# Large aggregations: products in PSUM and a sum by halves; sort turns in two banks

## The reference

```
x = x + gat0(layernorm(x), edges)        # 8 heads x 32
x = x + moe_small(layernorm(x), edges1)  # experts gated by a small 4 x 4 attention over 131072 edges
x = x + gat1(layernorm(x), edges)        # 4 heads x 64
x = x + moe(layernorm(x))                # 8 experts, the best 2 of each row
```

```
e     = leaky_relu(left[src] + right[dst], 0.2)         # (edges, heads)
p     = exp(e - segment_max(e, dst)[dst])
alpha = p / segment_sum(p, dst)[dst]
out   = segment_sum(table[src] * alpha[:, :, None], dst)  # (nodes, 256)
```

## Time and profile before

| what | value |
|---|---|
| median of three runs | 10248.09 us |
| profiled execution, own time | 10220.8 us |
| its span | 10218.8 us |
| busy: DVE (VectorE) / POOL (GpSimd) | 5655.7 us (55%) / 5738.3 us (56%) |
| busy: PE / ACT (ScalarE) | 2312.4 us (23%) / 1171.8 us (11%) |
| large aggregation 0 | 1000 to 3670 us of the span |
| small aggregation | 4232 to 5800 us |
| large aggregation 2 | 6306 to 8865 us |

### The profile page before, as it was taken

The page is one execution under the profiler, slowest core; times in us unless marked ns, Lnnn a source line. Parts: engine busy times, 40 slices in busy tenths (PEclk is TensorE's granted clock), DMA queues, the critical chain, the costliest instruction groups (busy, mean ns, idle before and its releaser), DMA issues. The chain is left out here.

```text
span 10218.8 us, 56607 instructions
## 1 busy us (share of the span) xinstructions
PE 2312.4 (23%) x9111; PEld 1766.1 (17%) x9112; DVE 5655.7 (55%) x8530; ACT 1171.8 (11%) x2978; POOL 5738.3 (56%) x5411
## 2 busy tenths in 40 slices
PE   0112000000000012256555421000000000029995
PEld 0111000000000001145444311000000000026663
DVE  8764688898777667333333474666656465431111
ACT  0101001000000001022222101000000000002221
POOL 0026667677777754545555446777777777542221
PEclk9555555555555555577777755555555555559997
DMA  1052333433333363311111253343343333530004
GB/s 33 0 154 61 91 83 90 119 100 101 99 100 99 93 125 60 113 27 33 28 28 28 69 151 101 103 121 106 108 120 104 111 100 102 123 111 30 30 30 116
DMA packets 485751, 869.30 MB, mean 85 GB/s; under 512 B 202782, under 2 KB 322508, under 8 KB 475840
## 3 DMA queue, kind: packets, MB, share of 16 engines
q0 software_dynamic: 239536, 575.99, 22.6%
q1 hardware_dynamic: 178976, 148.53, 5.3%
q10 hardware_dynamic: 67108, 143.54, 4.2%
HBM read 693.35 MB, written 180.71 MB: 86 GB/s over the span
## 5 line engine op out<-in xcount | busy, mean ns | idle before, releaser
L891 POOL DMA_INDIRECT agg_ring<-table,agg_idx x4320 | 4675.1, 1082 | 2070.6 <-issue 1316.7
L1022 DVE TENSOR_TENSOR agg_part<-agg_ring,agg_prob 128x2048 f32 x420 | 960.9, 2288 | 160.5 <-DVE agg_wide L1058 76.1
L1058 DVE TENSOR_TENSOR agg_wide<-agg_wide,agg_part 128x2048 f32<-128x2048 f32 x420 | 962.7, 2292 | 14.4
L1036 DVE TENSOR_TENSOR agg_score<-agg_el,agg_er 128x576 f32<-128x576 f32 (+1 forms) x98 | 59.8, 610 | 1268.9 <-issue 661.9
L1389 PE MATMUL agg_hp<-agg_xt,agg_w 128*128 128x256 f32 x1600 | 462.5, 450 | 555.7 <-ACT agg_ht L1359 267.4
L2205 DVE TENSOR_TENSOR experts_h<-experts_sg,experts_hp 128x682 f32<-128x682 f32 x106 | 91.8, 866 | 779.4 <-ACT experts_sg L2188 779.4
L2155 PE MATMUL experts_hp<-mixture_w,experts_xt 128*128 x1696 | 517.8, 457 | 0.6 <-ACT experts_xt L2184 0.6
L2126 POOL DMA_INDIRECT yc<-experts_ysb,experts_list x105 | 103.9, 990 | 684.3 <-DVE experts_ysb L2214 684.3
L1389 PEld LDWEIGHTS agg_hp<-agg_xt,agg_w 128*128 128x128 f32 x1600 | 361.3, 229 | 643.6 <-issue 298.5
L1403 PE MATMUL agg_yp<-agg_w,agg_ht 128*128 128x256 f32 x1600 | 408.0, 414 | 231.1 <-remote 141.4
L1962 PE MATMUL agg_weights_turned<-all_ident,agg_n 128*128 128x128 f32 x192 | 48.5, 406 | 1677.1 <-issue 827.3
(11 more groups left out here) (418 smaller groups left out, 6360.8 us busy)
## 6 DMA issues: line engine op xcount, KB each, us to landing
agg_ring<-table,agg_idx POOLq DMA_INDIRECT x4320
y<-agg_ysb ACTq DMA_DIRECT2D x25, 1024.0 KB
rank_y<-y SPq DMA_DIRECT2D x10, 2560.0 KB
rank_x<-x SPq DMA_DIRECT2D x30, 640.0 KB
copies<-first_sort_words SPq DMA_DIRECT2D x16, 1024.0 KB
copies<-last_sort_words ACTq DMA_DIRECT2D x16, 1024.0 KB
x<-rank_x SPq DMA_DIRECT2D x20, 640.0 KB
agg<-agg_res ACTq DMA_DIRECT2D x98, 128.0 KB
```

The lines of the kernel that those rows point to most:

```text
L891: pool.indirect_dma_start(out=self.ring[:, at:at + self.RW], out_offset=None, in_=self.table, in_offset=bass.IndirectOffsetOnAxis(ap=self. ...
L1022: return dve.tensor_tensor(to[:, :].rearrange("p (j h c) -> p j h c", j=UNIT, h=H), ring[:, ds(st.at(at_u), UNIT * RW)].rearrange("p (j w) ...
L1058: dve.tensor_tensor(wide[:, :], wide[:, :], part[:, :], ALU.add).then_inc(widened, 1)
```

## The change

- `part`, the product of a unit, is allocated in PSUM (2048 columns, four banks).
- The reduce L1063 over the 8 slots of `wide` becomes three additions in place of halves: 1024, 512 and 256 columns, each waiting for the one before (`quartered`, `halved`).
- To make room, the turn buffer of the sorts beside aggregation 0 has 1024 columns (two banks). A group of a turn that goes to a bank for the second time waits for the copy of the group two before. `prob` gets one bank in aggregation 2 (288 + 4 columns) and keeps two in aggregation 0 (576 + 8).
- The sort beside ranking 1 and the first sort keep their 2048 columns.

```diff
--- before.py
+++ after.py
@@ -138,6 +138,7 @@
         self.steps = sort_steps(log_part, log_free)
         self.bufs, self.turned, self.sign, self.ident = bufs, turned, sign, ident
         self.cmp_done, self.in_psum, self.copied = cmp_done, turned_in_psum, copied
+        self.window = self.F
         self.at = []
         n, cur = 0, 0
         for s in self.steps:
@@ -207,14 +208,16 @@
             if nturn:
                 pe.wait_ge(self.copied, nturn * self.ngroups)
             src = self.bufs[cur]
-            for first, end in self.groups():
-                if s[0] == "turn":
-                    for b in range(first // P, end // P):
-                        mm = pe.transpose(self.turned[:, b * self.PB:(b + 1) * self.PB], src[0:self.PB, b * P:(b + 1) * P],
+            for i, (first, end) in enumerate(self.groups()):
+                if first >= self.window:
+                    pe.wait_ge(self.copied, nturn * self.ngroups + i + 1 - self.window // 512)
+                for b in range(first // P, end // P):
+                    at = b % (self.window // P)
+                    if s[0] == "turn":
+                        mm = pe.transpose(self.turned[:, at * self.PB:(at + 1) * self.PB], src[0:self.PB, b * P:(b + 1) * P],
                                           self.ident[0:self.PB, 0:self.PB])
-                else:
-                    for b in range(first // P, end // P):
-                        mm = pe.transpose(self.turned[0:self.PB, b * P:(b + 1) * P], src[:, b * self.PB:(b + 1) * self.PB],
+                    else:
+                        mm = pe.transpose(self.turned[0:self.PB, at * P:(at + 1) * P], src[:, b * self.PB:(b + 1) * self.PB],
                                           self.ident[:, :])
                 mm.then_inc(self.in_psum, 1)
 
@@ -225,11 +228,12 @@
             dst = self.bufs[cur ^ 1]
             for i, (first, end) in enumerate(self.groups()):
                 act.wait_ge(self.in_psum, nturn * self.ngroups + i + 1)
+                back = first // self.window * self.window
                 if s[0] == "turn":
-                    a, b = first // P * self.PB, end // P * self.PB
-                    act.activation(dst[:, a:b], self.turned[:, a:b], ACT.Copy).then_inc(self.copied, 1)
+                    a, b, off = first // P * self.PB, end // P * self.PB, back // P * self.PB
+                    act.activation(dst[:, a:b], self.turned[:, a - off:b - off], ACT.Copy).then_inc(self.copied, 1)
                 else:
-                    act.activation(dst[0:self.PB, first:end], self.turned[0:self.PB, first:end], ACT.Copy).then_inc(self.copied, 1)
+                    act.activation(dst[0:self.PB, first:end], self.turned[0:self.PB, first - back:end - back], ACT.Copy).then_inc(self.copied, 1)
 
 
 class ListSort:
@@ -404,7 +408,7 @@
         shares = [5] * (2 * NSEARCH) + [14] * NG
         cuts = [0] * (len(shares) + 1)
         if after:
-            after.so.turned = s.ps("words_turned", [P, 2048])
+            after.so.turned, after.so.window = s.ps("words_turned", [P, 2048]), 2048
             cuts = [done + (len(after.so.steps) - done) * sum(shares[:i]) // sum(shares) for i in range(len(shares) + 1)]
         if zero:
             zero.allocate(s)
@@ -904,9 +908,9 @@
 
     def allocate(self, s):
         if self.parts:
-            turned = s.ps("words_turned", [P, 2048])
+            turned = s.ps("words_turned", [P, 1024])
             for ls, lo, hi, first, last in self.parts:
-                ls.so.turned = turned
+                ls.so.turned, ls.so.window = turned, 1024
 
     def begin_vector(self, dve):
         for ls, lo, hi, first, last in self.parts:
@@ -972,13 +976,14 @@
         sizes = s.sb("sizes", [1, 4 * NT], I32)
         er, m, bm, mn = s.sb("er", [P, H]), s.sb("m", [P, H]), s.sb("bm", [P, H]), s.sb("mn", [P, H])
         el, score, negs, zeros = s.sb("el", [P, SW]), s.sb("score", [P, SC + H]), s.sb("negs", [P, SW]), s.sb("zeros", [P, 1])
-        wide, part, summed = s.sb("wide", [P, UC]), s.sb("part", [P, UC]), s.sb("summed", [P, CW])
+        wide, part, summed = s.sb("wide", [P, UC]), s.ps("part", [P, UC]), s.sb("summed", [P, CW])
         acc, den, dsum, res, junk = s.sb("acc", [P, CW]), s.sb("den", [P, H]), s.sb("dsum", [P, H]), s.sb("res", [P, CW]), s.sb("junk", [P, 1])
-        prob = s.ps("prob", [P, 1024])
+        prob = s.ps("prob", [P, -(-(SC + H) // 512) * 512])
         const, sized, begun, hidden = s.sem("const"), s.sem("sized"), s.sem("begun"), s.sem("hidden")
         blank, copied, front, back = s.sem("blank"), s.sem("copied"), s.sem("front"), s.sem("back")
         added, leaked, topped, raised, lowered, kept = [s.sem(n) for n in ("added", "leaked", "topped", "raised", "lowered", "kept")]
         scored, probs, tail, widened = s.sem("scored"), s.sem("probs"), s.sem("tail"), s.sem("widened")
+        quartered, halved = s.sem("quartered"), s.sem("halved")
         scaled, folded, dens, combined = s.sem("scaled"), s.sem("folded"), s.sem("dens"), s.sem("combined")
         floored, inverted, tile_done, out_stored = s.sem("floored"), s.sem("inverted"), s.sem("tile_done"), s.sem("out_stored")
         beside.allocate(s)
@@ -1060,7 +1065,11 @@
                         dve.tensor_tensor(den[:, :], den[:, :], prob_scale, ALU.mult).then_inc(scaled, 1)
                         dve.tensor_tensor(acc3, acc3, prob_scale.unsqueeze(2).to_broadcast([P, H, C]), ALU.mult).then_inc(scaled, 1)
                         dve.wait_ge(widened, u1 + (cfg.RU + 1))
-                        dve.tensor_reduce(summed[:, :], wide[:, :].rearrange("p (j w) -> p w j", j=UNIT), AX.X, ALU.add).then_inc(folded, 1)
+                        dve.tensor_tensor(wide[:, 0:4 * CW], wide[:, 0:4 * CW], wide[:, 4 * CW:8 * CW], ALU.add).then_inc(quartered, 1)
+                        dve.wait_ge(quartered, kk)
+                        dve.tensor_tensor(wide[:, 0:2 * CW], wide[:, 0:2 * CW], wide[:, 2 * CW:4 * CW], ALU.add).then_inc(halved, 1)
+                        dve.wait_ge(halved, kk)
+                        dve.tensor_tensor(summed[:, :], wide[:, 0:CW], wide[:, CW:2 * CW], ALU.add).then_inc(folded, 1)
                         dve.wait_ge(scaled, kk * 3)
                         dve.tensor_tensor(den[:, :], den[:, :], dsum[:, :], ALU.add).then_inc(dens, 1)
                         dve.wait_ge(folded, kk)
```

## The result

The changed kernel takes 10309.1 us (7 runs, 10282 to 10327) against 10248.1 us (7 runs, 10223 to 10260): ratio 1.0061, 95% interval 1.0047 to 1.0076. It is slower by 0.6%, where I forecast 2% faster. The profiled execution's span went from 10218.8 to 10307.3 us.

What follows compares the result with a forecast made beforehand. POOL's gathers were taken to bound the two large aggregations. The ceiling's -313, ring-wait overshoot +112 and turns +4 gave -197 us from 10220.8, or 10024; the runs' median lying 27 us higher, 10050 us was forecast, range 9875 to 10225.

Steps and rivals of the forecast that it cites:

- part (a): Large aggregations: product in PSUM, so VectorE's addition no longer holds a gather; -487 us of POOL, VectorE's PSUM write taken as 0.
- Part (b): Sum over 8 slots as three additions: VectorE gains 118 us, held gathers cost POOL +88 us, bounds 0 and 225.
- Part (c): Long sort beside the first large aggregation: two-bank turns expose bank hand-overs, +4 us, at most 7.
- The ceiling: Large aggregations: below about 1.41 us per gather other sequencers slow; 3456 gathers take 4873 us, gain at most 313 us.
- backlog model: Each gather adds 1.41 us to a queue, passing time drains it; backlog over 2.25 us predicted slow ScalarE copies in 87%.
- rival 1: Gathers in the large aggregations are freed in full, the ceiling doesn't bind; 9870 us, chance 0.20.
- s: Queue work each gather adds, 1.41 us; 1.39 to 1.43 was said to give 9980 to 10150 us.
- the overshoot: Large aggregations: ring waits outlast the queue's draining by 3.3 us each, 34 waits, +112 us above 4873 us.
- rival 3: ScalarE's chain becomes the pace of the aggregations, slow tiles costing 9.4 us each; 10330 to 10510 us, chance 0.11.
- The sign to watch: Growth of VectorE's idle time at scoring line L1036, 909.5 us in the second aggregation, would point to ScalarE's chain as pace.

Runs made afterwards that it cites:

- e6: Kernel before with the reduce as three additions, tile sizes kept as 16-bit integers; kind Q, 9555.4 us, 1.006 of the kernel before.
- e14: Changed kernel with ScalarE copying only the first unit's scores of a chunk, the rest left out; kind P, 10106.9 us, 0.981 of the kernel before.
- e17: Changed kernel with POOL clearing an unread tile after every fourth large-aggregation gather and ScalarE copying two units at a time; kind P, 10084.5 us, 0.984 of kernel before.
- e15: Changed kernel with POOL also clearing an unread 128x400 tile after every fourth gather of the large aggregations; kind P, 10148.8 us, 0.991 of the kernel before.
- e2: Kernel before with the three additions, plus three masking register operations a tile and engine; kind P, 10335.9 us, 1.010 of the unmasked kernel before.
- e0: Changed kernel plus three masking register operations a tile and engine; kind P, 10425.9 us, 1.018 of the unmasked kernel before.
- e5: Changed kernel with tile sizes kept as 16-bit integers; kind Q, 9110.0 us, 0.959 of the kernel before.
- e18: Changed kernel with tile sizes kept as 16-bit integers; kind P, 10321.1 us, 1.007 of the kernel before.
- e9: Changed kernel with tile sizes kept as 16-bit integers, another run; kind Q, 9110.3 us, 0.960 of the kernel before.

## Why the prediction was wrong

**What held.** POOL set the pace before, and part (a) did what it says: no gather of over 1.1 us under L1063, 451 us where 487 were forecast. POOL's own time without ring waits is 3395 + 531 + 559 = 4485 us, where the prediction had 4512; so the error lies in the waits alone. Part (b): under the additions a gather takes longer. e6 measured 61 us where I had 88; how much VectorE's gain takes off in it was not separated.

```profile
7428.17 1.22 DVE L1068 TENSOR_TENSOR agg_wide<-agg_wide 128x1024 f32<-128x1024 f32 x1
7428.68 1.54 POOL L895 DMA_INDIRECT agg_ring<-table,agg_idx  x1 [0.30 <-issue]
```

By the Trainium skill ("SBUF — State Buffer", "Who interferes with whom") a VectorE instruction with two SBUF inputs contends with a GpSimd instruction that reads SBUF; this gather, which takes its indices from SBUF and is held 0.6 us under the addition of two SBUF tensors, agrees. VectorE's write to PSUM costs 8 ns (2296 for 2288), my 0. Part (c), +4 us in my sum and 7 at most, was not tried alone. On kind Q the turns take 2 us more than in e6. On kind P those of the changed kernel take 41 us more than before, though in the turn shown by ScalarE's lateness, which is the same trouble as in its copy loop, and not by the hand-over of banks that I had priced.

**The ceiling held in part.** 1.41 us per gather was worked out from the trace before. e14 and e17, so different in what they do, both come to 1.405 us in the second aggregation. In the first they stand at 1.50 us each (2588.0 and 2595.9 us), and no run says why it is more there. Nor do two kernels show that 1.405 can't be undercut: what holds e14 there is, by the rows above, VectorE's crawling loop. The same backlog model, fed with the gathers of the changed kernel, tells quick from slow copy intervals there in 98.6% of the cases with 1.42 us (82% in the first). On kind Q there is no such ceiling. So rival 1 is what the change does on the other kind of chip, and it fails on this one. One sum of the prediction is off: s from 1.39 to 1.43 gives 9980 to 10120 us around the forecast, not 10150. It changes neither the forecast nor the range.

**The step that failed** is the overshoot: "There are 26 such waits now [...] 361 us would be 34. [...] the queue is already empty for perhaps half: 3.3 x 34 = +112 us". Measured in place of 361 + 112 = 473 us of ring waits: 779 us, in 77 waits. In place of +112 us above the ceiling of 4873 us the gathers took 5263, +390. The length of a wait was right in the mean (10.1 us for the 10.7 taken); their number was not, 77 for 34, and 35 of them last over 10 us, 19.6 us in the mean. The overshoot comes to 390/77 = 5.1 us a wait where I took 3.3, or 11 us for each long one. The timeline shows how a long one is made. I let a ring wait end when VectorE gives entries back, 6.5 us after ScalarE's exponentials, and took ScalarE as ready. In the stop shown it is not: it is in the middle of a crawling copy loop when POOL stops, and needs 13 us more, and VectorE 10 us after it. POOL stands 23 us in it, and afterwards it issues at full rate again, into the next backlog. In the second aggregation tiles of 27 to 37 us stand between ones of 42 to 80 us, over and over. Quick tiles between slow ones are nothing new (22 of the 48 intervals between scorings were under 44 us before, 17 are now); the many long stops are.

That is in the main rival 3's mechanism, ScalarE's chain as the pace of the slow tiles, to which I gave 0.11. My argument against it ("the queue drains, and the next tiles are quick") is true, as the alternation shows, but was no relief. My reading, which no run tests, is that the ring is too small for it: it holds 96 slots, under three tiles, so what a quick tile gains POOL cannot bank. Its price was too high (10330 at the least, measured 10309). The sign to watch that I named for it, L1036's idle time, hardly moved (909.5 to 918.2 us); what moved was its releaser, and the ring waits.

**Why slower than before, and not merely equal.** Before, every addition held one gather for 1.16 us, in the midst of a chunk. This may have worked as the clearing does in e15: POOL rests a little all through the chunk, and not in one stop of 23 us. Two pairs of runs speak for it. Freeing the gathers (with the two-bank turns; e2 to e0, both masked) costs 90 us on kind P and gains 445 us on kind Q (e6 to e5). Putting a brake back elsewhere (e15) takes 1.6% off. That the old additions helped as a brake, and not in another way, is the nearest explanation, but it was not tried by itself.

**Open.** What makes a chip one of kind P. The gathers' durations and VectorE's instructions are the same on both kinds; the register operations of ScalarE, and in e14 of VectorE, are not. Why removing the loop (e14) and barely quickening it (e15) both help so much is known only as far as the ring waits above. The share of the loss outside the two aggregations (11 us of the 88) was not looked into.

## What to carry to other kernels

Work taken off the engine that paces a ring is worth its time only if the consumer's chain keeps up at the new pace; look at how long the chain takes in its worst tile, not at its mean, and at whether the ring can hold a tile's lead. Where register operations take ten times their usual time, count a loop by its sequencer instructions, look again for the crawling on the next engine once one loop is cured, and try a brake on the producer. Before trusting a gain of a few per cent, run it on more than one chip: here the same edit is -4.1% on one kind and +0.6% on the other.

## What the runs showed of the hardware

Two kinds of chip run the same program over 7% apart (9494 and about 10250 us), with equal durations of gathers (0.946 to 0.949 us at the median) and of VectorE's products. Of the 1201 us between the spans of e18 (P) and e9 (Q), 664 lie between the first and last gathers of the two large aggregations and 380 in the small one. On kind P, gathers issued every 1.25 us go with register operations of ScalarE of 0.69 us in place of 0.069, and still do so 13 us after the last one; on kind Q the longest is 80 ns at the same rate of gathers. With ScalarE's loop taken away, VectorE's register operations reach 0.69 us instead (e14). The lowest average that a kernel of this study reached on kind P is 1.405 us a gather, in the second aggregation. On kind P three more register operations a tile and engine cost 1.1% of the whole kernel.
